# Attention terms as columns of the node products, and separate buffers for the right relational weights

## The chip, the core and the metric

The kernel runs on one core of a Trainium2 chip. The metric is the time of one execution on the device in microseconds (us). The engines are PE (TensorE, matrix products; PEld its weight loads), DVE (VectorE), ACT (ScalarE), POOL (GpSimd) and SP (SyncE, which here only issues DMAs). All engines work side by side from instruction queues of their own and wait for each other by semaphores.

## The reference

Four graph layers follow one another on 6250 nodes with 128 features and 100000 edges sorted by destination; after each the input is added and the rows are normalised.

```
x = layernorm(x + L0(x))            # sum over edges, two linear layers
x = layernorm(x + L1(x))            # attention, two layers:
    h = x @ W_node + b_node
    for l in 0, 1:
        g = h @ lyr_W[l]
        s = (g * att_src[l]).sum(-1);  d = (g * att_dst[l]).sum(-1)
        e = leaky_relu(s[src] + d[dst])          # src, dst with a loop for each node
        h = softmax-weighted sum over edges of g[src] + lyr_bias[l]
x = layernorm(x + L2(x))            # relational, R = 4 relations, H = 4 heads, H * C = 512:
    xl = einsum('nf,rfh->nrh', h, W_l) + b_l     # "left"
    xr = einsum('nf,rfh->nrh', h, W_r) + b_r     # "right"
    e_feat = edge_attr @ W_e[r, :16] + rel_emb[r] @ W_e[r, 16:]     # r = type of the edge
    score = (leaky_relu(xl[src, r] + xr[dst, r] + e_feat) * att[r]).sum(-1)
    softmax over edges, sum of messages, feed-forward layer
x = layernorm(x + L3(x))            # graph convolution
```

## The kernel before, in words

The nodes are 49 blocks of 128 (`NB` = 49, `NP` = 6272 padded nodes), each block with nodes on the 128 partitions. The program is a series of stages (`nc.Block()`); in each, every engine gets a piece of code of its own, and a barrier stands between stages: the next one begins when the slowest engine of the last is through, waits for its DMAs included. Nothing reorders instructions; each engine runs them as they are written.

The attention layers. `gat_input` computes h: `cols_tensor` transposes the rows of x block by block into two PSUM banks, DVE (`cols_vector`, L410) and ACT (`cols_scalar`, L417) copy the groups of four alternately into `cols`, then PE multiplies 49 blocks by W_node (L426) and DVE adds the bias (L709). `gat_nodes`, called for each of the two layers, does the same with h and the layer's weights, ACT copying the products out (L434). Then DVE multiplies g by one attention vector (L761) and sums each row (L764), and again for the other vector: four passes over 6272 columns. SP stores g to the table in HBM (L735, rows of 130 elements of which 128 are g), and once DVE has made the `tail` (a one and the term s, L766) a second DMA stores these two columns (L737). `split_vector` (L1049, L1052) splits d into three bf16 parts. `gat_edges` then gathers table rows for 1664 pairs of an edge tile and a node block (POOL, L810), and `gat_layer` mixes the sums with g.

The relational tables. `rel_tables` makes two tables in HBM, left and right, each with 49 blocks of 4 x 516 columns: per relation 512 columns of the product and 4 of a linear term (the product with attention already summed over a head). Per block PE does four products of 512 columns (L1142, five banks in turn) and a small one (L1147), DVE adds the bias into one of two row buffers `rel_out` (L1249, L1252), and SP stores the buffer (L1110); DVE waits for the store of two blocks earlier before it writes. The left and the right side use the same SBUF places `wl` and `bl` for weights and biases. ACT's queue loads them (L1160, L1161): the left ones after the gates' exponential, the right ones when all left blocks are through and after the **attribute chain**, a loop over 16 edge features in which ACT loads one row of `edge_attr`, casts it to three bf16 parts (L1179) with POOL taking the remainders (L1120), and stores four rows (L1164). Before its first block DVE prepares small things: three-part splits of attention and edge weights, `rel_wide`, the softmax of the gates, the type rows (L1226, L1231), and the linear terms of weights and bias (L1236, L1238). Between the sides it adds four folded rows to the right bias (L1223; PE's L1133) and makes the linear terms again.

The gathers that read both tables (L1702) belong to the next stage, whose first DMA issue is SP's L1719.

## Time and profile before

| what | value |
| --- | --- |
| median of 3 executions | 10470.95 us (10433.81 to 10505.31) |
| the profiled execution | 10493.45 us, of which the span from first to last instruction is 10491.6 us |
| busy | PE 5383.1 us (51%), PEld 3542.6 (34%), DVE 5196.6 (50%), ACT 1919.2 (18%), POOL 5653.5 (54%) |
| granted TensorE clock, mean | 0.697 of full speed |

A row of the timeline has the start in us from the start of the span, the duration in us, the engine (PEq, ACTq, SPq for what a queue issues), the line of the program, the operation, what it writes and reads, and how many of them are merged into the row; in square brackets stands the idle time before it and what ended it. The page of the profile says that matmuls are pipelined and their ends modelled, and that a few matmul records can be missing.

### The profile page before, as it was taken

Reading aid. Unit: us, or ns where it says so; the run is one execution under the profiler, and the core shown is the slowest. Engines: PE = TensorE matmul, PEld = TensorE weight load, DVE = VectorE, ACT = ScalarE, POOL = GpSimd, SP = SyncE. Lnnn points to the kernel's source line nnn. Section 1 sums busy time; section 2 is a strip of 40 time slices with the busy share of each in tenths; the row PEclk is TensorE's granted clock in tenths of the full one; section 3 lists DMA queues with packets and bytes.
Section 4 is the critical chain, followed back from the end, with each engine's and each line's share of the span. In section 5 each row is a group of like instructions: output and inputs, shape, how many; then the busy total and the mean of one; then the engine's idle time right before and its main releaser. Section 6 shows DMA issues by size and latency. Waiting matters only on the chain. (4 is left out here: it accounts for less than half of the span.)

```text
span 10491.6 us, 95206 instructions
## 1 busy us (share of the span) xinstructions
PE 5383.1 (51%) x23693; PEld 3542.6 (34%) x23809; DVE 5196.6 (50%) x19168; ACT 1919.2 (18%) x4711; POOL 5653.5 (54%) x5712
## 2 busy tenths in 40 slices
PE   2333423333332333337777777777767777723333
PEld 2332312223231232223322222222236767613233
DVE  3232443333352333356667777777766666623225
ACT  0000111111111111111022222222224444410000
POOL 6666235555426555521066666666656666356663
PEclk5555655555565555558888898899988888855555
DMA  2111021121121122117566666666656666311111
GB/s 62 46 46 47 20 46 50 54 56 53 54 46 52 55 56 56 53 34 280 231 210 204 201 207 206 202 201 204 202 156 175 176 175 175 94 49 46 46 46 35
DMA packets 445514, 1155.74 MB, mean 110 GB/s; under 512 B 117604, under 2 KB 159172, under 8 KB 431928
## 3 DMA queue, kind: packets, MB, share of 16 engines
q0 software_dynamic: 295984, 849.83, 28.2%
q1 hardware_dynamic: 133660, 272.06, 7.7%
q10 hardware_dynamic: 15340, 27.77, 0.8%
q8 instruction: 213, 3.49, 0.1%
q14 instruction: 317, 2.60, 0.1%
HBM read 1016.71 MB, written 132.52 MB: 110 GB/s over the span
## 5 line engine op out<-in xcount | busy, mean ns | idle before, releaser
L810 POOL DMA_INDIRECT gat_ring<-gat_table,psrc_idx x1664 | 1604.6, 964 | 1804.8 <-PE bank L863 674.3
L863 PE MATMUL bank<-gat_ring,gat_hot 128*128 128x130 f32 x3328 | 759.6, 397 | 1092.2 <-DVE gat_hot L968 707.9
L565 DVE TENSOR_TENSOR acc<-acc,bank 128x129 f32 (+1 forms) x1664 | 479.0, 288 | 1540.2 <-remote 811.4
L1702 POOL DMA_INDIRECT pair<-right_table,idx_r_idx x782 | 799.7, 1023 | 654.9 <-POOLq L1095 217.5
L979 DVE TENSOR_TENSOR acc<-acc,bank 128x130 f32 x1664 | 481.3, 289 | 1225.3 <-remote 682.0
L1852 POOL DMA_INDIRECT msg<-left_table,pidx_idx x832 | 814.4, 979 | 495.5 <-PE bank L1926 203.9
L863 PEld LDWEIGHTS bank<-gat_ring,gat_hot 128*128 128x128 f32 x3328 | 648.8, 286 | 1197.2 <-DVE gat_hot L968 701.7
L1702 POOL DMA_INDIRECT acc<-left_table,idx_l_idx x782 | 804.5, 1029 | 452.0 <-issue 228.7
L511 POOL DMA_INDIRECT gcn_sum_ring<-gcn_table,src_idx x782 | 761.2, 973 | 391.3 <-issue 220.5
L511 POOL DMA_INDIRECT gin_sum_ring<-in_x,src_idx x782 | 761.1, 973 | 381.5 <-issue 221.8
L1764 ACT ACTIVATE positive<-acc 128x512 f32<-128x512 f32 x782 | 492.5, 630 | 2121.1 <-DVE acc L1792 1415.9
L1741 PE MATMUL bank<-pair,ident 128*128 128x512 f32 x1564 | 869.1, 639 | 0.7
L537 PE MATMUL bank<-gcn_sum_ring,gcn_sum_hot 128*128 x1664 | 425.8, 430 | 759.4 <-issue 305.8
L1792 DVE TENSOR_TENSOR acc<-acc,bank 128x512 f32<-128x512 f32 x782 | 532.1, 681 | 479.7 <-remote 233.5
L537 PE MATMUL bank<-gin_sum_ring,gin_sum_hot 128*128 x1664 | 415.8, 422 | 664.0 <-issue 273.1
L1804 DVE CUSTOM_DVE_ANT_0 positive<-positive,bank 128x128 f32<-128x128 f32 x3128 | 711.9, 277 | 42.4 <-issue 38.9
L1738 PE MATMUL bank<-edge_w,feat 128*128 128x512 bf16 x2254 | 680.7, 411 | 49.4 <-DVE acc L1792 23.4
L537 PEld LDWEIGHTS bank<-gcn_sum_ring,gcn_sum_hot 128*128 128x128 f32 x1664 | 357.8, 313 | 827.3 <-issue 826.0
L537 PEld LDWEIGHTS bank<-gin_sum_ring,gin_sum_hot 128*128 128x128 f32 x1664 | 350.4, 307 | 729.3 <-issue 728.3
L833 PE MATMUL bank<-gat_d_parts,gat_spread 128*128 x1664 | 207.9, 184 | 622.1 <-DVE gat_spread L891 333.1
L875 ACT ACTIVATE gat_ring<-gat_ring,gat_wt 128x129 f32<-128x129 f32 x1664 | 491.4, 389 | 3.4 <-issue 2.3
L870 ACT ACTIVATE gat_wt<-gat_sl 128x52 f32<-128x52 f32 x32 | 7.9, 246 | 2621.1 <-DVE gat_ratio L950 2308.8
(499 smaller groups left out, 9587.3 us busy)
## 6 DMA issues: line engine op xcount, KB each, us to landing
gat_place<-local_rows SPq DMA_DIRECT2D x128, 416.0 KB
left_table<-rel_out SPq DMA_DIRECT2D x49, 1032.0 KB, 5.0
right_table<-rel_out SPq DMA_DIRECT2D x49, 1032.0 KB, 3.9
feat<-attr_rows SPq DMA_DIRECT2D x194, 256.0 KB
gat_ring<-gat_table,psrc_idx POOLq DMA_INDIRECT x1664
types<-type_rows SPq DMA_DIRECT2D x98, 256.0 KB
msg<-left_table,pidx_idx POOLq DMA_INDIRECT x832
gin_sum_ring<-in_x,src_idx POOLq DMA_INDIRECT x782
```

What stands on the lines that cost most here:

```text
L511: e.indirect_dma_start(ring[:, at:at + F], None, table[:, :], bass.IndirectOffsetOnAxis(ap=ed["src"][:, i:i + 1], axis=0)).then_inc(*got[b ...
L537: e.matmul(k.psum[j % NBANK][:, 0:width], hot[b % NH][:, j % Q * P:(j % Q + 1) * P], ring[:, bass.ds(at[j % BATCH], width)], start=True, s ...
L810: e.indirect_dma_start(ring[:, at:at + TROW], None, table[:, :], bass.IndirectOffsetOnAxis(ap=ed["psrc"][:, i:i + 1], axis=0)).then_inc(*g ...
L863: e.matmul(k.psum[i % NBANK][:, 0:TROW], hot[i // HQ % NH][:, i % HQ * P:(i % HQ + 1) * P], ring[:, at:at + TROW], start=True, stop=True). ...
L875: e.mul(row, row, wt[:, i % CT:i % CT + 1]).then_inc(*scaled.up())
L1702: e.indirect_dma_start(to[j % NG][:, n * LROW:(n + 1) * LROW], None, tab[:, :], bass.IndirectOffsetOnAxis(ap=idx[:, i:i + 1], axis=0)).the ...
L1738: e.matmul(x, m, edge_w[:, q * LROW:q * LROW + HC], start=(q == 0), stop=False)
L1741: e.matmul(x, c["ident"][:, :], side(rights, i), start=False, stop=True).then_inc(*edge_made.up())
L1764: e.activation(positive[i % NA][:, :], side(lefts, i), ACT.Relu, scale=0.8).then_inc(*relued.up())
L1792: e.tensor_tensor(xs, xs, k.psum[bank_x[i % NX]][:, 0:HC], ALU.add).then_inc(*summed.up())
L1804: d = e.tensor_tensor_reduce(out=pos[:, s], in0=pos[:, s], in1=k.psum[bank_a[at % NE]][:, s], scale=1.0, scalar=0.0, op0=ALU.mult, op1=ALU ...
L1852: e.indirect_dma_start(rows[j % NG][:, n * LROW:(n + 1) * LROW], None, left[:, :], bass.IndirectOffsetOnAxis(ap=ed["pidx"][:, i:i + 1], ax ...
```

## The change

In the attention layers the input product disappears as a stage: in layer 0 a folded matrix `whole` = W_node x [lyr_W, 0, lyr_W a_src, lyr_W a_dst] is made on chip (a transposition, two small products and copies), and x itself is multiplied by it. In both layers the two attention terms are columns of the same product, which has 131 columns for a block (`GROW`: g, a one from the `base` row, s, d). Products go into four banks in groups of three blocks, DVE moves them out with the base row added, and SP stores each group of three blocks with all 130 columns when it is out. The four passes, the ACT copies and the tail are gone. `gx` takes the place of `h` and has rows of 131 elements; the later passes read g, s and d out of it.

In `rel_tables` the right weights and biases get buffers of their own, those of the softmax of the next stage (`soft`), and SP's queue loads them at the start. The left weights are issued by ACT as its first instructions, left bias and attention row by SP as its first. DVE makes the left linear terms and begins with the blocks; everything else that it prepared stands now between the blocks (`between`), at the block numbers written there, and the two sides follow each other without a gap.

```diff
-                e.wait_ge(*taken.at(len(GROUPS)))
-                e.dma_start(tv[:, :, 0:F], blocks3(g)).then_inc(*stored.up(16))
-                e.wait_ge(*tailed.at(1))
-                e.dma_start(tv[:, :, F:TROW], t3).then_inc(*stored.up(16))
-                e.wait_ge(*stored.at(2, 16))
+                for j, (lo, hi) in enumerate(THREES):
+                    e.wait_ge(*taken.at(j + 1))
+                    e.dma_start(tv[lo:hi].rearrange("b p f -> p b f"), g3[:, lo:hi, 0:TROW]).then_inc(*stored.up(16))
+                e.wait_ge(*stored.at(len(THREES), 16))
...
+                if layer == 0:
+                    e.wait_ge(*loaded.at(len(loads), 16))
+                    e.transpose(k.psum[4][:, 0:P], wn[:, :], c["ident"][:, :]).then_inc(*wn_turned.up())
+                cols_tensor(e, k, c, x, turned, out_v, out_s, xw)
+                e.wait_ge(*widened.at(1))
+                if layer == 0:
+                    e.matmul(k.psum[5][:, 0:GROW], bn[:, :], wx[:, :], start=True, stop=True)
+                    e.matmul(k.psum[4][:, P:P + GROW], wn[:, :], wx[:, :], start=True, stop=True).then_inc(*folded.up())
+                    e.wait_ge(*whole_in.at(1))
...
+                for j, (lo, hi) in enumerate(THREES):
+                    if j >= 4:
+                        e.wait_ge(*taken.at(j - 3))
+                    for b in range(lo, hi):
+                        m = e.matmul(k.psum[j % 4][:, (b - lo) * GROW:(b - lo + 1) * GROW], cols[:, b * P:(b + 1) * P],
+                                     weight[:, :], start=True, stop=True)
+                    m.then_inc(*product.up())
...
-                for j in (0, 1):
-                    e.wait_ge(*dve.now())
-                    e.tensor_tensor(blocks3(cols), blocks3(g), att[:, j * F:(j + 1) * F].unsqueeze(1).to_broadcast(
-                        [P, NB, F]), ALU.mult).then_inc(*dve.up())
-                    e.wait_ge(*dve.now())
-                    e.tensor_reduce(nd(j), blocks3(cols), AX_X, ALU.add).then_inc(*dve.up())
+                e.wait_ge(*loaded.at(len(loads), 16))
...
+                cols_vector(e, k, cols, turned, out_v)
...
+        weight = [by_r(wl), [b[:, :] for b in (soft.near01, soft.near, soft.far, soft.pen)]]
+        bias = [by_r(bl), [b[:, :] for b in (soft.val, soft.top, soft.tot, soft.ex)]]
...
+                for dst, src in first_loads:
+                    e.dma_start(dst, src).then_inc(*firsts.up(16))
                 for dst, src in loads:
                     e.dma_start(dst, src).then_inc(*loaded.up(16))
+                for dst, src in later_loads:
+                    e.dma_start(dst, src).then_inc(*laters.up(16))
...
-                    for r in range(R):
-                        e.dma_start(wl[:, r * HC:(r + 1) * HC], w[wn][r]).then_inc(*weights.up(16))
-                    e.dma_start(bl[:, :], broadcast_row(w[bn].rearrange("r f -> (r f)"))).then_inc(*weights.up(16))
...
+                def between(n):
+                    if n == 1:
+                        e.wait_ge(*loaded.at(len(loads), 16))
+                        e.tensor_copy(part(0, SLOTS), typ_i).then_inc(*typed.up())
+                        e.wait_ge(*typed.now())
+                    if n == 2:
+                        gates()
+                    if 3 <= n < 3 + R:
+                        is_type(n - 3)
+                    if n == 8:
+                        split_vector(e, att_f[0:R, 0:HC], att_f[0:R, HC:2 * HC],
+                                     lambda j: att_parts[0:R, j * HC:(j + 1) * HC], dve, att_split)
...
+                    for r in range(R):
+                        if n == FOLD(r) + 1:
+                            e.wait_ge(*laters.at(2 * R, 16))
+                            e.wait_ge(*fold.at(r + 1))
+                            e.tensor_tensor(bias[1][r], bias[1][r], k.psum[7][:, 0:HC], ALU.add).then_inc(*folded.up())
+                        if n in (FOLD(r) + 2, FOLD(r) + 3):
```

Here `FOLD(r)` is 20 + 5r, and n counts the blocks of both sides, 0 to 97.

How the order on the engines moves is seen at three places. The first is DVE from the end of the normalisation before the attention layers to the first instruction of the edge stage of layer 0. Before:

```order
L410 COPY gat_in_cols<-bank 128x512 x6
L410 COPY gat_in_cols<-bank 128x128
L709 TENSOR_TENSOR gat_h<-bank,gat_in_b 128x512 x12
L709 TENSOR_TENSOR gat_h<-bank,gat_in_b 128x128
L685 UNCONDITIONAL_BRANCH
L753 UNCONDITIONAL_BRANCH
L755 MEMSET gat_tail 128x98
L410 COPY gat_cols<-bank 128x512 x6
L410 COPY gat_cols<-bank 128x128
L761 TENSOR_TENSOR gat_cols<-gat_h,gat_att 128x6272
L764 TENSOR_REDUCE gat_node<-gat_cols 128x49
L761 TENSOR_TENSOR gat_cols<-gat_h,gat_att 128x6272
```

After the change, from the first instruction of the node stage on (`ISA` is the reduction of a product of two rows, with the store of its sum):

```order
L749 COPY gat_whole<-gat_bn 128x128
L751 COPY gat_wn<-bank 128x128
L752 COPY gat_bn<-gat_whole 128x128
L755 ISA gat_scratch,gat_w<-gat_w,gat_att 128x128
L755 ISA gat_w 128x1
L755 ISA gat_scratch,gat_w<-gat_w,gat_att 128x128
L755 ISA gat_w 128x1
L413 COPY gat_cols<-bank 128x512 x6
L413 COPY gat_cols<-bank 128x128
L761 TENSOR_TENSOR gat_base<-gat_base,bank 128x131
L762 COPY gat_whole<-bank 128x131
L766 TENSOR_TENSOR gat_g<-bank,gat_base 128x393 x16
```

The seven copies, thirteen additions and the four full passes of the input and node stages have gone; seven copies and seventeen additions out of PSUM stay, and in front of them stand the preparations. The second place is SP in the same node stage of layer 0, first before, then after:

```order
L733 DMA gat_w<-in_L_gnn_lyr_W 128x128
L733 DMA gat_att<-in_L_gnn_att_src 128x128
L733 DMA gat_att<-in_L_gnn_att_dst 128x128
L733 DMA gat_bias<-in_L_gnn_lyr_bias 128x128
L735 DMA gat_table<-gat_h 128x49x128
L737 DMA gat_table<-gat_tail 128x49x2
```

```order
L707 DMA gat_w<-in_L_gnn_lyr_W 128x128
L707 DMA gat_att<-in_L_gnn_att_src 128x128
L707 DMA gat_att<-in_L_gnn_att_dst 128x128
L707 DMA gat_bias<-in_L_gnn_lyr_bias 128x128
L707 DMA gat_wn<-in_L_gnn_W_node 128x128
L707 DMA gat_bn<-in_L_gnn_b_node 128x1
L710 DMA gat_table<-gat_g 128x3x130 x16
L710 DMA gat_table<-gat_g 128x130
```

The two stores behind everything have become 17, one for each group of three blocks, and there are two more loads. The third place is DVE at the start of the relational tables, from the column copies on. Before:

```order
L1204 TENSOR_REDUCE gate<-gate 128x1
L1206 TENSOR_SCALAR gate<-gate 128x4
L1208 TENSOR_REDUCE gate<-gate 128x1
L1210 RECIPROCAL gate<-gate 128x1
L1212 TENSOR_SCALAR gate<-gate 128x4
L1214 TENSOR_SCALAR gate<-gate 128x4
L1226 CAST attr_parts<-rel_out 128x896
L1231 TENSOR_SCALAR attr_parts<-attr_parts 128x896 x4
L1236 TENSOR_TENSOR rel_out<-rel_wl,att_all 128x2048
L1238 TENSOR_REDUCE w_lin<-rel_out 128x16
L1236 TENSOR_TENSOR rel_out<-rel_bl,att_all 128x2048
L1238 TENSOR_REDUCE b_lin<-rel_out 128x16
```

After:

```order
L413 COPY acc<-bank 128x512 x6
L413 COPY acc<-bank 128x128
L1267 TENSOR_TENSOR rel_out<-rel_wl,att_all 128x2048
L1268 TENSOR_REDUCE w_lin<-rel_out 128x16
L1267 TENSOR_TENSOR rel_out<-rel_bl,att_all 128x2048
L1268 TENSOR_REDUCE b_lin<-rel_out 128x16
L1282 TENSOR_TENSOR rel_out<-bank,rel_bl 128x512 x4
L1285 TENSOR_TENSOR rel_out<-bank,b_lin 128x4x4
L1228 CAST attr_parts<-soft_code 128x896
L1282 TENSOR_TENSOR rel_out<-bank,rel_bl 128x512 x4
L1285 TENSOR_TENSOR rel_out<-bank,b_lin 128x4x4
L1210 TENSOR_REDUCE gate<-gate 128x1
```

Between the column copies and the first block only the linear terms are left; type rows and gates stand behind blocks 0, 1, 2 and so on. At the change of sides DVE had, before, the rows L1223 to L1238 below between block 48 and block 49:

```order
L1249 TENSOR_TENSOR rel_out<-bank,rel_bl 128x512 x4
L1252 TENSOR_TENSOR rel_out<-bank,b_lin 128x4x4
L1223 TENSOR_TENSOR rel_bl<-rel_bl,bank 128x512 x4
L1236 TENSOR_TENSOR rel_out<-rel_wl,att_all 128x2048
L1238 TENSOR_REDUCE w_lin<-rel_out 128x16
L1236 TENSOR_TENSOR rel_out<-rel_bl,att_all 128x2048
L1238 TENSOR_REDUCE b_lin<-rel_out 128x16
L1249 TENSOR_TENSOR rel_out<-bank,rel_bl 128x512 x4
L1252 TENSOR_TENSOR rel_out<-bank,b_lin 128x4x4
```

Those pieces stand now singly behind blocks 20 to 37, and the first right block follows the last left one.

## Rows read from the trace of the kernel before

**Rows 1.** Timeline around layer 0's input and node stages; columns as explained above.

```profile
1382.56 0.33 SPq L688 DMA_DIRECT2D gat_in_b<-in_L_gnn_b_node  x1
...
1415.32 11.46 PE L426 MATMUL bank<-gat_w,gat_cols 128*128 128x128 f32 x98 [0.43 <-DVE gat_cols L410]
...
1427.33 6.69 DVE L761 TENSOR_TENSOR gat_cols<-gat_h,gat_att 128x6272 f32<-128x6272 f32 x1 [12.11 <-ACT gat_h L434]
...
1464.43 29.83 SPq L819 DMA_DIRECT2D gat_place<-local_rows  x6
```

**Rows 2.** Timeline, node stage of layer 1 and the passes ahead of it.

```profile
3042.60 6.68 DVE L1028 TENSOR_TENSOR acc<-acc,gat_node 128x6272 f32<-128x6272 f32 x1
...
3063.01 0.33 SPq L733 DMA_DIRECT2D gat_w<-in_L_gnn_lyr_W  x1
...
3064.18 0.69 DVE L410 COPY gat_cols<-bank 128x512 f32<-128x512 f32 x1 [0.93 <-PE bank L402]
...
3073.42 0.29 DVE L410 COPY gat_cols<-bank 128x128 f32<-128x128 f32 x1 [0.42 <-PE bank L402]
...
3085.82 0.38 SPq L735 DMA_DIRECT2D gat_table<-gat_h  x1
...
3122.66 12.65 SPq L819 DMA_DIRECT2D gat_place<-local_rows  x5
```

**Rows 3.** Timeline of the relational tables, edges and change of sides.

```profile
4739.27 1.31 SPq L1099 DMA_DIRECT2D score<-in_L_gnn_W_e  x2
...
4753.54 0.41 DVE L1049 CAST att_parts<-score 4x512 bf16<-4x512 f32 x1 [3.57 <-DMA rel_out<-in_recs]
...
4762.56 0.17 DVE L1214 TENSOR_SCALAR gate<-gate 128x4 f32<-128x4 f32 x1
...
4770.24 6.16 PE L1142 MATMUL bank<-rel_wl,acc 128*128 128x512 f32 x8 [20.59 <-DMA rel_bl<-in_L_gnn_b_l]
...
4774.18 2.28 DVE L1236 TENSOR_TENSOR rel_out<-rel_wl,att_all 128x2048 f32<-128x2048 f32 x1
...
4774.66 0.47 ACTq L1173 DMA_DIRECT2D score<-in_attr  x1
...
4784.98 2.48 DVE L1249 TENSOR_TENSOR rel_out<-bank,rel_bl 128x512 f32<-128x512 f32 x4
...
4976.63 0.17 DVE L1252 TENSOR_TENSOR rel_out<-bank,b_lin 128x16 f32<-128x16 f32 x1
...
5018.06 1.79 ACTq L1160 DMA_DIRECT2D rel_wl<-in_L_gnn_W_r  x4
...
5045.28 2.48 DVE L1249 TENSOR_TENSOR rel_out<-bank,rel_bl 128x512 f32<-128x512 f32 x4
...
5224.90 0.16 DVE L1252 TENSOR_TENSOR rel_out<-bank,b_lin 128x16 f32<-128x16 f32 x1
5229.51 0.60 SPq L1719 DMA_DIRECT2D types<-type_rows  x1
```

**Rows 4.** Windows: stretch, length, busy by engine, PEclk, DMA share, GB/s.

```profile
3067.00:3068.00 1.00, 1.00 (x6) 0.97 (x7) 0.02 (x1) 0.52 (x1) 0.00 (x0) 0.50 0.27 22
3102.00:3103.00 1.00, 0.00 (x0) 0.00 (x0) 1.00 (x1) 0.00 (x0) 0.00 (x0) 0.50 0.53 84
4765.00:4767.00 2.00, 0.00 (x0) 0.00 (x0) 0.00 (x0) 0.00 (x0) 0.00 (x0) 0.50 1.00 385
4785.00:4881.00 96.00, 92.74 (x245) 42.97 (x246) 63.63 (x124) 15.20 (x19) 20.05 (x12) 0.98 0.89 340
5137.00:5225.00 88.00, 87.38 (x240) 41.61 (x238) 67.38 (x122) 0.00 (x0) 0.00 (x0) 1.00 0.70 289
```

**Rows 5.** DMA to landing, tiles left_table, then right_table (in the tables' stage).

```profile
DMA to landing us min/median/max: 3.9/5.0/8.5
...
DMA to landing us min/median/max: 3.9/3.9/5.3
```

**Rows 6.** DMA issues, 4739 to 4785: count, KB each, median us to landing.

```profile
type_rows<-attr_parts ACTq DMA_DIRECT2D x5, 224.0 KB, 1.9
```

More of the change, by code:

```diff
@@ L33 @@
 LROW = HC + H
+GROW = F + 3
 LAG = 3
@@ L989, in _, with gat_layer @@
                     sums(cn)
-def gat_layer(k, c, ed, w, layer, g, x, acc, table, local_rows):
+def gat_layer(k, c, ed, w, layer, gx, x, acc, table, local_rows):
     name = f"gat{layer}"
@@ L997, in gat_layer @@
         stat = k.sb("ln1_stat", 3 * NB, ctx=own)
-        gat_nodes(k, c, w, layer, g, node, d_parts, bias, table)
+        gat_nodes(k, c, w, layer, gx if layer else x, gx, node, d_parts, bias, table)
         gat_edges(k, c, ed, name, acc, table, local_rows, d_parts)
         acc3, nd = blocks3(acc, ROW), lambda j: node[:, j * NB:(j + 1) * NB]
-        s, d, has, loop, high, w_loop, w_sum, total = (nd(j) for j in range(8))
+        g3 = blocks3(gx, GROW)[:, :, 0:F]
+        s, d = (blocks3(gx, GROW)[:, :, F + j] for j in (1, 2))
+        has, loop, high, w_loop, w_sum, total = (nd(j) for j in range(2, 8))
         dve, compared, exped = k.begin("dve", "compared", "exped")
```

392 lines of the change are left out of this document (193 added, 199 removed).

## Prediction, made before the changed kernel was run

> **What bounds the kernel now.** I read the row of busy times first, then the timeline at the edges of the stages, then windows and landing times. Over the whole span of 10491.6 us no engine is busy more than 54% of the time (the table of the section on time and profile): the kernel is a line of stages, each closed by a barrier, and a stage's length is set by its own last wait. The page's chain of waits covers only the last stage, so it says nothing about these two places, and they have to be read from the timeline. The profiled execution took 10493.45 us against a median of 10470.95; the sum below is made against 10493.45 and carried over to the median as a ratio.
>
> Three stretches are touched. **First**, input product and node stage of attention layer 0: from SP's first issue at 1382.56 to the first issue of the edge stage at 1464.43, 81.9 us [rows 1]. The reader is to see that after the last product VectorE makes four full passes of 6.69 us, the first at 1427.33, and only then can SP store the last two columns, in pieces of 8 bytes; the stage ends some 10 us after that. **Second**, the same node stage of layer 1: 3063.01 to 3122.66, 59.7 us [rows 2]. **Third**, the relational tables: 4739.27 to 5229.51, 490.2 us [rows 3]. There the left side's 49 blocks run from 4784.98 to 4976.8, 3.91 us each, and the right side's from 5045.28 to 5225.07, 3.67 each. Before the first block stand 45.7 us, and between the sides 68.5 us in which VectorE and TensorE mostly idle: the right weights may only be fetched (5018.06) when ScalarE's chain over the edge attributes is through, because the same engine queues both and the weights go into the place of the left ones.
>
> **Part 1, attention layers.** Removed: the whole input product, the four passes (4 x 6.69 = 26.8 us on the path, both layers), the ScalarE copies and the tail store. Added: loads ahead of the column copies (VectorE waits for them before its first copy), two reductions of 128 columns, in layer 0 a transposition and a fold of two matrices, three more columns in each product, and 17 stores instead of two. What the store waits for is new: it may begin after three blocks and then runs beside the products.
>
> Layer 0, step by step. Four loads issued from 3063.01 had their traffic over by about 3067.6 (the window 3067 to 3068 still shows a share of 0.27, [rows 4]): 4.6 us. Two more cost some 0.9 us, so the weights are in at 1382.56 + 5.5 = 1388.1. Transposing, copying and the two reductions are seven short instructions in a line, at 0.17 to 0.41 us each [rows 3] some 2.2 us: 1390.3. From the first column copy to the last takes 3073.42 - 3064.18 = 9.24 us [rows 2] and 0.36 more to the first product: 1399.9. The fold adds two small matmuls, two evictions and two handoffs, 1.2 us: 1401.1. Products: 98 half products in 11.46 us [rows 1], times 131/128, 11.7 us; three blocks take 0.72 us and their eviction of 393 columns 0.56 (0.69 us for 512 columns, 0.29 for 128, [rows 2]), so TensorE still sets that pace. The first store goes out 1.3 us after the first product, at 1402.4. Now the store: the single one of layer 1 was issued at 3085.82 [rows 2] and its traffic ended within the window 3102 to 3103 [rows 4], 16.7 us. That is longer than the 11.7 us of the products, so **the store is what comes late next**: 1419.1, plus 2.4 us from the end of traffic to the next stage (4.4 us from the last right block to 5229.51, less 2 us of data, [rows 3]): 1421.5. Gain 1464.43 - 1421.5 = **43 us**.
>
> Layer 1 has no fold and four loads: 3067.6 + 0.9 = 3068.5 for the first copy (4.3 us later than now), 3078.1 first product, 3079.4 first store, 3096.1 end of traffic, 3098.5 next stage. Gain 3122.66 - 3098.5 = **24 us**. Together 67 us. Bounds: 75 if the products set the end instead of the store (2 x 5 us less, some of it lost in the last landing), 57 if loads and fold take 5 us more in each layer. The later elementwise passes read rows 131 elements apart instead of 128; a pass over `acc`, whose rows are 130 apart, takes what the others do (6.68 and 6.69 us, [rows 2]), so I put that at nothing.
>
> The Trainium skill (SBUF — State Buffer, The DMA setup-cost knee) speaks against the 17 stores: each transfer pays a roughly fixed 2 us, so one should send the largest single transfer. By the fit that it gives, 195 KB would take 2.5 us and 17 of them in a line 42 us, an estimate; overlap between stores in one queue decides it, and the rows of this stage show no two stores in flight of this size, so neither case is ruled out by them.
>
> **Part 2, relational tables.** Three things move. (a) *The start.* VectorE's work before the first block was 9.2 us of splits and gates (4753.54 to 4762.7) after 3.57 us of waiting, then a wait for weights until 4770.1, then 4.1 us of type rows, then 10.8 us of linear terms [rows 3]. Now only the linear terms stay, four passes of 2.29 us, and the left weights are issued first. 3.1 MB have to be in (weights, biases, attention row); at the 385 GB/s of [rows 4] that is 8.1 us after a first issue near 4740, 4750.4 with the landing, about when the column copies end (4749.97: the cast at 4753.54 had waited 3.57 us). First eviction at 4750.5 + 4 x 2.29 + 0.3 = 4760.0 instead of 4784.98: **25 us**. (b) *The gap between the sides* of 68.5 us goes altogether, if the right weights are in: they are issued before the first table store. (c) *What comes back.* The attribute chain starts when block 6 does, near 4783 instead of 4774.66, and needs about 250 us (243.4 us for its sixteen features now, the last three without company, [rows 3]), so it ends near 5035. Blocks beside it cost 3.91 us, blocks without it 3.67: the share of the DMA engines is 0.89 in the one window and 0.70 in the other [rows 4], the landing of a table store 5.0 us against 3.9 in the middle [rows 5]. That makes 70 blocks at 3.91 and 28 at 3.67, 376.5 us, against 371.6 for all 98 now: 5 us back. The work moved between the blocks is 9.2 + 2.2 us from the start, and for the right terms 4 x (0.69 + 4 x 0.69) = 13.8 us: 25 us of VectorE in about 20 pieces of at most 2.8 us. Its cover is the wait for the store two blocks back: a block holds 2.65 us of VectorE work in 3.91. Pieces of 1.4 us hide but for some 0.2, the three of 1.6 to 2.8 us stick out by about 1.5 each; with four fold matmuls of 1.1 us on TensorE I charge 5 us. If the cover were gone it would be the full 25 us and 4.4 more.
>
> SP has three small stores put ahead of block 10's; they are issued while SP waits for that block anyway. ScalarE waits for the gates until block 2, and behind that wait stands the attribute chain, counted under (c). POOL's part of that chain follows it and holds nobody else: the next stage's gathers wait for the barrier.
>
> Sum: blocks end at 4760.0 + 376.5 + 5 = 5141.5, the next stage begins 4.4 us later at 5146, against 5229.51: **83 us**. Bounds 58 (cover gone) and 92 (no inserts seen, chain not slower).
>
> Total 67 + 83 = **150 us**: 10493.45 - 150 = 10343.5, or 1.43%. On the median: 10470.95 x (1 - 150/10493.45) = **10321 us**.
>
> **Rivals.**
> *The work between blocks is not covered.* For it: left blocks already wait on stores, so a late VectorE makes a late store, and the loop over two buffers passes it on. Against it: 1.26 us free in each block. It costs 25 + 4.4 - 5 = 24 us more: gain 126, 10345 us. Chance 0.12.
> *The 17 stores follow one another.* A small store of 224 KB landed in 1.9 us [rows 6]; with 0.38 us to issue, 17 x 2.28 = 38.8 us instead of 16.7, 22 us in each layer: gain 106, 10365 us. Against it: the loads at the start of the third stretch are issued two in 1.31 us, without waiting for each other [rows 3], and such loads flow at 385 GB/s [rows 4]. This is where the skill's rule would lead. Chance 0.06.
> *More is gained.* The products and not the store end the node stages, and the chain slows fewer blocks: 75 + 92 = 167 and up, 10304 us. Chance 0.09.
> *Slower than before.* Place: the loop over the two row buffers. A pair of blocks takes landing + issue + VectorE's 2.65 us; at 5.0 us that is (5.0 + 0.32 + 2.65)/2 = 3.98 each, as seen. If the new company (right weights, the chain, short pieces) raised the landing of every table store to the 8.5 us of the slowest one now [rows 5], it would be 5.7 us a block, 562 us for 98, 185 more than the 377 above: 35 us slower than before, 10506 us. It decides against the change from a landing of 7.8 us on. Against it: the same bytes are written at the same rate, and the extra 2 MB of weights are in before the second block. Chance 0.03.
> *The change does not do what it says*, in that the right side still waits: its wait is for weights landed 200 us earlier and terms made ten blocks earlier, so this has no price that I can find and is held in the last case.
>
> **How the numbers follow.** Forecast 0.70, the rivals as given. Single executions of this kernel lie from 10433.81 to 10505.31, 0.35% about the median, so about 1% is what a measurement can tell from no change. The forecast's own range is 125 to 175 us; with the scatter of 0.3% on top and the first three rivals inside it, 10275 to 10380. Faster by over 1% needs 105 us: all of the forecast save its edge, most of the first rival, half of the second: 0.85. Within 1%: 0.12. Slower: 0.03.
>
> **What would show it.** After it the edge stage of layer 0 begins near 1421, 39 us after the stage's first issue; VectorE has no pass of 6.69 us between products and edges; store traffic runs unbroken for about 17 us. The node stage of layer 1 is about 35.5 us long. The first eviction of the left table stands 21 us after the stage's first issue, the 98 blocks run without a gap and the stage is 407 us long. Wrong would be: a traffic record with holes between the 17 stores, blocks 8 to 14 and 20 to 38 longer than their neighbours by more than 1 us, or a first column copy later than 8 us into the node stages.

## The result, and the profile after

The changed kernel takes 10348.08 us (median of 4 executions, 10303.08 to 10355.34) against 10472.08 us (median of 4) for the kernel before: a ratio of 0.9874 with a 95% interval of 0.983 to 0.9918, that is 124 us or 1.26% faster. The interval is clear of 1. The forecast was 10321 us, faster by over 1% with a chance of 0.85. The profiled execution took 10344.3 us (the sum of the prediction, made against 10493.45, gave 10343.5).

Busy times from the page of the changed kernel, against the table of the section on time and profile:

```profile
span 10342.5 us, 94979 instructions
PE 5314.2 (51%) x23667; PEld 3474.6 (34%) x23667; DVE 5146.7 (50%) x19201; ACT 1901.7 (18%) x4679; POOL 5637.5 (55%) x5712
```

They say as little as before: 69 us less work on PE and 50 on DVE, and 149 us less span. The timeline at the edges of the stages tells more. Node stage of layer 0, to be laid beside [rows 1] (columns as there):

```profile
1377.09 0.33 SPq L707 DMA_DIRECT2D gat_w<-in_L_gnn_lyr_W  x1
1382.82 0.22 DVE L749 COPY gat_whole<-gat_bn 128x128 f32<-128x128 f32 x1 [5.32 <-issue]
1384.48 0.69 DVE L413 COPY gat_cols<-bank 128x512 f32<-128x512 f32 x1
1393.92 0.29 DVE L762 COPY gat_whole<-bank 128x131 f32<-128x131 f32 x1
1394.26 11.21 PE L730 MATMUL bank<-gat_whole,gat_cols 128*128 128x131 f32 x98 [0.59 <-DVE gat_whole L762]
1395.31 10.75 DVE L766 TENSOR_TENSOR gat_g<-bank,gat_base 128x393 f32<-128x393 f32 x17 [1.10 <-PE bank L730]
1395.90 13.59 SPq L710 DMA_DIRECT2D gat_table<-gat_g  x17
```

The four passes of 6.69 us are gone; products, evictions and the issuing of 17 stores run side by side. The edge stage begins at 1415.62: 38.5 us after the first issue, where it was 81.9. Windows of the same stretch (after the busy times: clock, DMA share, GB/s):

```profile
1397.00:1412.00 15.00, 8.47 (x76) 8.28 (x75) 8.82 (x20) 0.00 (x0) 0.00 (x0) 0.85 1.22 201
1413.00:1414.00 1.00, 0.00 (x0) 0.00 (x0) 0.00 (x0) 0.00 (x0) 0.00 (x0) 0.50 0.46 86
1414.00:1416.00 2.00, 0.00 (x0) 0.00 (x0) 0.00 (x0) 0.36 (x1) 0.00 (x0) 0.50 0.03 7
```

Store traffic starts within 1396 to 1397 and ends within 1413 to 1414, about 17 us, and the stage ends 2 us later. (A share above 1 can't be right, so I use the GB/s.) Layer 1, beside [rows 2]:

```profile
3028.20 0.33 SPq L707 DMA_DIRECT2D gat_w<-in_L_gnn_lyr_W  x1
3033.26 0.06 DVE L747 MEMSET gat_w<- 128x1 f32 x1 [4.65 <-DMA gat_bias<-in_L_gnn_lyr_bias]
3033.90 0.69 DVE L413 COPY gat_cols<-bank 128x512 f32<-128x512 f32 x1
3045.42 12.85 SPq L710 DMA_DIRECT2D gat_table<-gat_g  x17
3065.23 0.81 SPq L822 DMA_DIRECT2D gat_place<-local_rows  x2
```

37.0 us long. Relational tables, beside [rows 3]:

```profile
4710.77 0.33 SPq L1114 DMA_DIRECT2D rel_bl<-in_L_gnn_b_l  x1
4722.76 0.29 DVE L413 COPY acc<-bank 128x128 f32<-128x128 f32 x1 [0.42 <-PE bank L404]
4725.01 2.29 DVE L1267 TENSOR_TENSOR rel_out<-rel_wl,att_all 128x2048 f32<-128x2048 f32 x1 [1.95 <-DMA rel_wl<-in_L_gnn_W_l]
4734.30 2.48 DVE L1282 TENSOR_TENSOR rel_out<-bank,rel_bl 128x512 f32<-128x512 f32 x4
4736.95 0.33 SPq L1130 DMA_DIRECT2D left_table<-rel_out  x1
4933.15 5.90 SPq L1130 DMA_DIRECT2D right_table<-rel_out  x2
5010.52 4.15 ACTq L1180 DMA_DIRECT2D attr_rows<-attr_parts  x4
5118.17 0.59 SPq L1752 DMA_DIRECT2D types<-type_rows  x1
```

407.4 us long. There is no gap between the sides: the first right store stands 196.2 us after the first left one, which is 49 blocks of 4.00 us. One block stands out. The prediction named blocks 8 to 14 longer than their neighbours by more than 1 us as a sign of being wrong, and block 8 is: its store follows that of block 7 by 8.08 us, where each of the four distances before is 3.66.

```profile
4762.76 0.32 SPq L1130 DMA_DIRECT2D left_table<-rel_out  x1
4770.84 0.32 SPq L1130 DMA_DIRECT2D left_table<-rel_out  x1
```

What VectorE did there is read further down. All stretches of the two profiled executions, from the first DMA issue of one to that of the next:

| stretch | before | after | difference | forecast |
| --- | --- | --- | --- | --- |
| up to the first attention stage (not touched) | 1382.6 | 1377.1 | -5.5 | 0 |
| input and node stage, layer 0 | 81.9 | 38.5 | **-43.3** | -43 |
| edges and mixing, layer 0 (row distance only) | 1598.6 | 1612.6 | +14.0 | 0 |
| node stage, layer 1 | 59.7 | 37.0 | **-22.6** | -24 |
| edges, mixing and norm, layer 1 (row distance only) | 1616.6 | 1645.5 | +28.9 | 0 |
| relational tables | 490.2 | 407.4 | **-82.8** | -83 |
| the rest (not touched) | 5262.1 | 5224.3 | -37.8 | 0 |

The three touched stretches give 148.7 us. The open question is in the other rows. Are the 43 us more in the edge stages and the 38 us less behind the tables scatter, or do they belong to the change?

### The profile page after: what moved, and what is told of

Read it like the earlier page. It is cut to its first block and busy times, and to the rows that moved or that the text cites. A ratio compares the mean times of both kernels' runs of the same rounds, so it can differ in the third digit from the quotient of the medians.

```text
span 10342.5 us, 94979 instructions
## 1 busy us (share of the span) xinstructions
PE 5314.2 (51%) x23667; PEld 3474.6 (34%) x23667; DVE 5146.7 (50%) x19201; ACT 1901.7 (18%) x4679; POOL 5637.5 (55%) x5712
## 5 line engine op out<-in xcount | busy, mean ns | idle before, releaser
L866 PE MATMUL bank<-gat_ring,gat_hot 128*128 128x130 f32 x3328 | 730.0, 385 | 975.6 <-DVE gat_hot L971 574.1
L866 PEld LDWEIGHTS bank<-gat_ring,gat_hot 128*128 128x128 f32 x3328 | 622.1, 275 | 1077.2 <-DVE gat_hot L971 572.4
L1837 DVE CUSTOM_DVE_ANT_0 positive<-positive,bank 128x128 f32<-128x128 f32 x3128 | 711.3, 278 | 40.7 <-issue 38.9
L1771 PE MATMUL bank<-edge_w,feat 128*128 128x512 bf16 x2346 | 705.3, 413 | 38.4 <-DVE acc L1825 24.9
```

What stands on the lines that cost most here:

```text
L866: e.matmul(k.psum[i % NBANK][:, 0:TROW], hot[i // HQ % NH][:, i % HQ * P:(i % HQ + 1) * P], ring[:, at:at + TROW], start=True, stop=True). ...
L1771: e.matmul(x, m, edge_w[:, q * LROW:q * LROW + HC], start=(q == 0), stop=False)
L1837: d = e.tensor_tensor_reduce(out=pos[:, s], in0=pos[:, s], in1=k.psum[bank_a[at % NE]][:, s], scale=1.0, scalar=0.0, op0=ALU.mult, op1=ALU ...
```

## The experiments

The runs were made in groups, each on one chip with the kernel before beside it: in the table the first four rows, the next four, the next three, and the last row alone. The first three groups fell on two chips on which the kernel before takes 8585 to 8597 us, the last on a third where it takes 10471 us, much as in the result above. So the runs are compared by stretches and by their own group's ratio. The stretches are in us, all from profiled executions; three runs have a single execution, so they are read by their traces alone:

| run | node 0 | edges 0 | node 1 | edges 1 | tables | rest | ratio (95% interval) |
| --- | --- | --- | --- | --- | --- | --- | --- |
| before again | 84.5 | 1141.0 | 61.5 | 1174.0 | 494.8 | 4419.3 | one execution, 8579.14 us |
| changed again | 40.9 | 1141.0 | 38.9 | 1175.8 | 413.0 | 4422.4 | 0.9822 (0.9807 to 0.9837) |
| attention part alone | 41.4 | 1141.6 | 40.2 | 1173.8 | 495.2 | 4421.2 | 0.993 (0.9917 to 0.9944) |
| tables part alone | 83.8 | 1143.7 | 61.6 | 1174.5 | 410.0 | 4430.1 | 0.9898 (0.9883 to 0.9914) |
| one store | 47.0 | 1141.6 | 46.5 | 1174.1 | 410.8 | 4425.8 | 0.9847 (0.9832 to 0.9862) |
| steps ahead of the blocks | 38.1 | 1140.1 | 36.4 | 1173.3 | 420.6 | 4432.8 | 0.9841 (0.9826 to 0.9856) |
| chain later | 38.4 | 1140.9 | 36.8 | 1172.3 | 454.4 | 4435.8 | one execution, 8484.05 us |
| half rows | 38.1 | 1140.1 | 37.3 | 1173.4 | 394.8 | 4427.5 | 0.981 (0.9796 to 0.9823) |
| no linear product | 37.5 | 1139.6 | 36.2 | 1173.2 | 399.0 | 4439.9 | one execution, 8434.56 us |
| columns first | 32.7 | 1138.6 | 31.4 | 1172.7 | 409.1 | 4433.0 | 0.9813 (0.98 to 0.9827) |
| columns first and half rows | 31.8 | 1136.9 | 31.7 | 1174.0 | 395.6 | 4427.3 | 0.9799 (0.9785 to 0.9812) |
| a pad in each block (slower chip) | 38.6 | 1595.1 | 37.7 | 1646.4 | 418.3 | 5220.7 | 0.9884 (0.9864 to 0.9905) |

### Does the change touch anything outside its three stretches?

The kernel before again, the changed kernel again, and each half of the change alone (only `rel_tables` exchanged between the two programs):

> The kernel before once more, for a second profile of it: how far do the stages that nobody touched scatter from one execution to the next? Theory A (the change acts in three stages alone): the edge stage of layer 0 with its mixing passes takes 1598.6 us or differs from that by as much as it did after the change (+14), the same for the edge stage of layer 1 (1616.6, +29 after the change) and for all that follows the tables (5262.1, -38 after the change). Rival B (the change also lengthens the edge stages, 43 us, and something gives it back later): both edge stages come within 5 us of the first profile, 1598.6 and 1616.6. The three touched stretches are to be 81.9, 59.7 and 490.2 us, within 1 us, by both.

> The changed kernel once more. Theory A: the three touched stretches repeat at 38.5, 37.0 and 407.4 us within 1 us each, and the untouched ones move by some 10 to 40 us without a pattern, so that 148.7 us of the three stretches against the 124 us between the medians is scatter. Rival B: edge stages at 1612.6 and 1645.5 again within 5 us, that is 43 us longer than before.

> The attention part alone: the node stages of the change with the relational tables of the kernel before. Theory A, parts add: 43.3 + 22.6 = 66 us faster than before, ratio 0.9937, tables stretch 490 us. Rival B, the attention part costs something in the edge stages (rows 131 apart, other places in the memory): 66 - 43 = 23 us faster, ratio 0.998.

> The relational part alone: the tables of the change with the node stages before. Theory A: 83 us faster, ratio 0.9921, node stretches 81.9 and 59.7 us as before. Rival B (later stages win 38 us from the tables part, by what they find in the memory or in the queues): 83 + 38 = 121 us, ratio 0.988.

On this chip the edge stages agree to 0.0 and 1.8 us between before and changed, 1141.04 against 1141.04 and 1174.02 against 1175.79. So neither the row distance of 131 instead of 128 nor anything else in the change costs more there than these 2 us. The touched stretches gain 43.6 + 22.5 + 81.8 = 148 us, what they gained on the other chip, and the medians 8596.75 - 8443.28 = 153.5 us. The halves add: 61.5 us and 88.0 us by their medians, 149.5 together, against 66 and 83 expected. My expectation that the three stretches repeat within 1 us was too narrow: they came out 1.9 to 5.6 us longer. The figures expected for the edge stages could not be met, since these stages are 440 to 460 us shorter on this chip, with either kernel. Rival B is out on this chip. On the slower chip the pad run below has 1595 us in the edge stage of layer 0, so the +14 us there are scatter. But it again has 1646 us in the edge stage of layer 1 and 5221 us behind the tables, as the changed kernel had and the kernel before not. With one profile of before at that speed I can't tell whether the +29 and -38 us belong to the change there. They cancel but for some 10 us.

### What ends the node stages?

One store of the whole table in place of 17 (the last wait, for one store instead of 17, is not shown):

```
-for j, (lo, hi) in enumerate(THREES):
-    e.wait_ge(*taken.at(j + 1))
-    e.dma_start(tv[lo:hi].rearrange(...), g3[:, lo:hi, 0:TROW])
+e.wait_ge(*taken.at(len(THREES)))
+e.dma_start(tv.rearrange("b p f -> p b f"), g3[:, :, 0:TROW])
```

> The changed kernel with one store of the whole table in each attention layer, after the last product, in place of 17. Theory A (the store is what ends the node stage, and its 17 pieces flow without a gap beside the products): the store goes out some 11 us later, right after the last product is taken, still takes some 17 us, and each node stage is 10 to 12 us longer, 20 to 24 us in all. Rival B (each transfer pays a fixed 2 us and the 17 pieces wait for one another): the single store moves its 3.3 MB in some 9 us at the 385 GB/s that loads reached, and the stages stay within 3 us or get shorter. By the Trainium skill (SBUF - State Buffer, The DMA setup-cost knee) the 17 pieces would need an estimated 42 us against some 10 us for the single one.

Timeline of that run, SP's queue:

```profile
1229.14 0.38 SPq L709 DMA_DIRECT2D gat_table<-gat_g  x1
1247.23 0.81 SPq L821 DMA_DIRECT2D gat_place<-local_rows  x2
```

The single store goes out 10.8 us after the first product was taken (1218.37) and the next stage begins 18.1 us later. With 17 stores the same distance, first store to next stage, is 19.7 us (1395.90 to 1415.62) and 19.8 us in layer 1. So the 3.3 MB take nearly the same time in one piece or in 17, and what 17 pieces buy is the earlier start: against the three other runs of this group, whose node stages are the change's (38.1 to 38.4 and 36.4 to 37.3), the stages are 8.6 to 8.9 and 9.2 to 10.1 us longer, a little under the expected 10 to 12. The pieces did not wait for one another. By the Trainium skill (SBUF — State Buffer, The DMA setup-cost knee), which gives each transfer a roughly fixed 2 us, 17 pieces in a line would have been the slower form by some 30 us, an estimate from its figures. The traces do not agree: 17 pieces took 19.7 us against 18.1, so in one queue the fixed parts overlap.

Then the loads. Their wait stood ahead of the column copies (5.3 us in layer 0, 4.65 in layer 1). Here the copies go first, and the widening stands between the fifth and the sixth of VectorE's (TensorE's part of the edit is not shown):

```
 def cols_vector(e, k, cols, turned, out_v, inside=None):
     for g, (lo, hi) in enumerate(GROUPS):
+        if inside and g == 10:
+            inside()                  # wait for the loads, widen the weights
```

> The changed kernel with the column copies of both attention layers ahead of the wait for the loads: VectorE copies five groups and widens the weights between the fifth and the sixth, TensorE transposes the node weight after group 8. Theory A (loads and copies then run side by side, and the chain up to the first product is what sets the first store, the stores' 17 us the end): first product some 4 us earlier in both layers, the stages 4 us shorter each, 8 us in all. Rival B (the copies' own pace is broken by the steps between them): under 2 us in all.

SP's queue in that run, layer 0:

```profile
1203.52 0.33 SPq L711 DMA_DIRECT2D gat_w<-in_L_gnn_lyr_W  x1
1217.08 13.05 SPq L714 DMA_DIRECT2D gat_table<-gat_g  x17
1236.19 0.81 SPq L830 DMA_DIRECT2D gat_place<-local_rows  x2
```

The first store goes out 13.6 us into the stage instead of 18.8, and the next stage begins 19.1 us behind it, near the 19.7 of the change. The stages are 32.7 and 31.4 us long, 4.8 us less each than in the run of its group whose node stages are the change's (37.5 and 36.2): theory A, with a little more than the 4 us expected.

### What sets the pace of the blocks?

The prediction took the round of two row buffers for it: a buffer is free again when its store has landed, so a block takes (landing + issue + VectorE's work) / 2. Four runs test this, three here and the pad of the next section. The first holds the attribute chain until the left side is done (ScalarE waits for the last left eviction ahead of `for f in range(DE)`):

> The changed kernel with ScalarE's chain over the edge attributes held until the left side's last block is done. Theory A (the chain is what makes a left block longer than a right one): left blocks fall from 3.98 to 3.74 us or below, right blocks rise to some 3.95 us; the chain then needs some 255 us from there and ends the stage, about 55 to 70 us later than now. Rival B (it is the left table, or its early loads): left blocks stay at 3.98 and right ones at 3.74.

The page's landings of the table stores in that run:

```profile
left_table<-rel_out SPq DMA_DIRECT2D x49, 1032.0 KB, 3.9
right_table<-rel_out SPq DMA_DIRECT2D x49, 1032.0 KB, 5.0
```

and the windows of a left stretch without the chain and a right one with it (busy PE, PEld, DVE, ACT, POOL, then clock, DMA share, GB/s):

```profile
3650.00:3790.00 140.00, 140.00 (x379) 65.98 (x378) 117.09 (x217) 0.00 (x0) 0.00 (x0) 1.00 0.69 285
3820.00:3900.00 80.00, 74.94 (x198) 34.35 (x198) 51.65 (x100) 12.16 (x15) 16.72 (x10) 0.98 0.87 334
```

The sides have changed roles: left 185.3 us (3.78 a block, with the steps between the blocks in it), landing 3.9; right 3.97 a block, landing 5.0. So the chain, not the side, makes a block slow. The stage grew by 44 us against the 410.8 of its group, not 55 to 70, since the chain alone took some 245 us, not 255. And the first window shows what I had not read: **TensorE is busy 140.00 of 140 us.** Without the chain the blocks are bound by TensorE. The kernel before had it in a row that stands ahead of the prediction: 87.38 of 88 us in its last window [rows 4].

To test that, the small product of the linear terms is left out of all blocks but two (`if n < 2:` ahead of it), and with it TensorE's wait for its bank and VectorE's wait for the product. The other blocks' linear columns are then read from products of block 0 or 1.

> The changed kernel without the 16-column product of the linear terms in all blocks but the first two (left out: the linear terms of the other blocks' rows, whose evictions read the product of block 0 or 1 again, so what stands in those columns of the tables is not the reference's). It takes some 0.3 us of TensorE's work out of each block and nothing of VectorE's, SP's or the stores'. Theory A (in blocks without company TensorE is what sets the pace, busy 100% of the window): right blocks fall from 3.64 us, where nothing runs beside them, to 3.35 to 3.5. Rival B (the prediction's account: the round of two row buffers sets it, (landing + issue + VectorE's work) / 2): 3.64 us stay.

SP's queue over the last right blocks, this run:

```profile
3900.09 88.73 SPq L1130 DMA_DIRECT2D right_table<-rel_out  x27
```

and its window there:

```profile
3905.00:3985.00 80.00, 79.82 (x187) 35.19 (x186) 62.82 (x120) 0.00 (x0) 0.00 (x0) 1.00 0.76 315
```

With the product, in the run with columns first, whose tables are those of the change, the queue:

```profile
3900.02 84.00 SPq L1138 DMA_DIRECT2D right_table<-rel_out  x24
```

and the window:

```profile
3905.00:3980.00 75.00, 75.00 (x207) 35.87 (x206) 57.38 (x104) 0.00 (x0) 0.00 (x0) 1.00 0.70 289
```

26 distances in 88.4 us are 3.40 us a block, 23 in 83.7 us are 3.64. Less work for TensorE makes a block 0.24 us shorter at the same buffers and the same stores: theory A. The round of the buffers, by the prediction's formula 3.44 us at the landing of 3.9 on this side, is then just as near, so 3.40 alone does not tell which of the two limits is left. Beside the chain the same cut brought little: the left side took 195.9 us against 199.3, that is 0.07 us a block, and TensorE was busy 128.73 of 140 us there (window 3640 to 3780).

The third gives the buffers more room: each row stored in two halves, from four half buffers in the same memory. The cut is shortened. Not shown are the small product, which moves ahead of the four others, its eviction, which is done in two, and the wait for one half buffer at a time.

```
+for half in range(2):
+    at = slice(half * 2 * LROW, (half + 1) * 2 * LROW)
     e.wait_ge(*biased...); e.wait_ge(*lin_biased...)
-    e.dma_start(tview[b], out_rows[n % 2][:, :])
+    e.dma_start(tview[b][:, at], out_rows[n % 2][:, at])
```

> The changed kernel with each block's row stored in two halves of two relations each (4 half buffers in the same memory, 196 stores of 516 KB in place of 98 of 1032 KB; the product of the linear terms goes ahead of the four others, its eviction is done in two). Theory A (the blocks are bound by the round of two buffers, landing plus VectorE's work, not by the rate of the DMA engines): a block comes near VectorE's own work, 3.0 to 3.4 us, and the stage is 50 to 85 us shorter. Rival B (writing at some 270 GB/s is what the memory takes beside the rest): within 5 us. Rival C (196 stores pay more fixed cost): some us longer.

The stage is 394.8 us long, 16 us shorter than its group's 410.8: neither A's 50 to 85 nor B's 5. The window of its left side:

```profile
3640.00:3780.00 140.00, 138.48 (x372) 64.00 (x371) 121.25 (x256) 23.60 (x28) 30.46 (x19) 1.00 0.95 353
```

TensorE is busy 99% beside the chain, where it was 97.31 of 100 us in the changed kernel and 96.32 in the one before (windows 4800 to 4900). The left side, beside the chain, gains most: 186.5 us against 199.2 in the run with one store, 0.26 us a block. Once the stores let go, TensorE's 3.64 us a block is what is left; 98 of them are 357 us, and this run's two sides take 186.5 + 180.9 = 367.4. I had expected VectorE's own work to be the floor; it is not the next limit. The run changed the order of the products too, and no run tells the two apart.

### Are the steps between the blocks covered?

VectorE's steps of blocks 1 to 19 ahead of block 0 (`for n in range(20): between(n)`):

> The changed kernel with VectorE's steps that stand between blocks 1 and 19 (the wait for all loads, gates, type rows, both splits) put ahead of the first block again. Theory A (between the blocks they hide behind the wait for the row buffer): the first table store comes 15 to 20 us later, the blocks take as long as before, and the stage is 12 to 18 us longer. Rival B (between the blocks they were not covered): the first blocks get shorter by what the start loses, and the stage is within 4 us of the changed kernel's.

The first table store comes 15.7 us later (40.8 us into the stage instead of 25.1), both sides together are 5.9 us shorter than in the run with one store, whose tables are unchanged (379.8 against 385.7), and the stage is 9.8 us longer, below the 12 to 18 expected. Part of the 5.9 us is another matter: the type rows are ready sooner, so the chain starts at +28 us instead of +44 and keeps company to fewer blocks. Only 1.2 us of the 5.9 are gained on the left side, where the steps had stood, and 4.7 on the right, where none had. So the run bounds the uncovered part of these steps at some 6 us but doesn't measure it, and it says nothing of the steps of blocks 20 to 37.

The run with the chain later shows all of them at once, without company. Its left side, from the first left store to the first right one, takes 185.3 us where 49 blocks of 3.66, the distance at which most of them stand, are 179.3. So the steps cost 6.0 us. Most of that is not VectorE's: the stores of blocks 20, 25, 30 and 35 each follow the one before by 4.81 us, and there TensorE makes a fold product between the blocks:

```profile
3686.91 1.12 PE L1158 MATMUL bank<-rel_we,rel_wide 8*128 8x512 f32 x2
```

Each of these groups of five blocks takes 1.1 us more than five times 3.66, so the four fold products come to 4.5 us, and everything else between the blocks to 1.5. TensorE was busy through the whole of that side (180.00 of 180 us, window 3617 to 3797).

Beside the chain it is another matter at block 8, where VectorE splits the attention row into three parts. In the changed kernel, with GpSimd's subtraction for the chain:

```profile
4762.58 1.66 POOL L1140 TENSOR_TENSOR score<-score,attr_parts 128x782 f32<-128x782 f32 x1 [218.08 <-ACT attr_parts L1195]
4762.60 1.91 DVE L1054 CAST att_parts<-score 4x512 bf16<-4x512 f32 x1
4765.27 1.87 DVE L1054 CAST att_parts<-score 4x512 bf16<-4x512 f32 x1
```

and with the chain later:

```profile
3643.70 0.40 DVE L1054 CAST att_parts<-score 4x512 bf16<-4x512 f32 x1
```

The split took 5.7 us instead of 2.7, and block 8's store came 8.08 us behind block 7's instead of 5.12. This is where the prediction's sign was seen, and it was there in all seven profiles that have the split beside the chain and rows stored whole (7.9 to 8.4 us). Blocks 20 to 38 can't be read this way: beside the chain neighbouring distances scatter from 2.5 to 7.1 us even in the kernel before, which has no steps there.

To measure the cover itself, one more VectorE pass in each of the 98 blocks:

```
+then(e.tensor_tensor(soft.parts[:, 0:256], att_all[:, 0:256], att_all[:, 0:256], ALU.mult))
 if n >= 2:
     e.wait_ge(*stored[n % 2].at(n // 2, 16))
```

> The changed kernel with one more VectorE product of 256 columns (nothing reads it) at the start of each of the 98 blocks, some 0.35 to 0.4 us with its wait, ahead of the wait for the row buffer. It is the cover of the steps between the blocks measured 98 times over. Theory A (TensorE sets 3.65 us a block where nothing else runs, the row buffer's round some 3.98 beside the chain; VectorE has 0.6 us free in either): the stage stays within 6 us of the changed kernel's 411 to 413 us. Rival B (steps between the blocks are not covered): 98 x 0.37 = 36 us longer, blocks at 4.0 and 4.3 us.

Windows of that run, a left and a right stretch:

```profile
4800.00:4900.00 100.00, 92.08 (x239) 41.34 (x238) 86.01 (x158) 16.02 (x19) 20.98 (x13) 0.98 0.85 325
5020.00:5100.00 80.00, 80.00 (x221) 38.15 (x219) 68.85 (x134) 0.00 (x0) 0.00 (x0) 1.00 0.71 292
```

The pad's own row among the groups of the right window:

```profile
L1275 DVE TENSOR_TENSOR soft_parts<-att_all 128x256 f32<-128x256 f32 x22 | 9.1, 416 | 0.0
```

The right side takes 185.2 us as without pads (185.0): where TensorE is busy 80.00 of 80 us, 0.42 us more of VectorE's work per block cost nothing. The left side takes 207.7 us, against 196.2 in the changed kernel's first profile and 199.2 to 200.4 in four others of the same tables on the faster chips: 0.15 to 0.23 us a block, a third to a little over half of the pad, and TensorE falls from 97 to 92%. Beside the chain the cover is partial; that a late store makes the next round late there is the likely reason. The stage took 418.3 us. That is 5 to 7 us over the 411 to 413 from which the expectation was made, at the edge of A's 6, and 10.9 over the 407.4 of the result's profile; both are far from B's 36.

### The version the runs point to

> Columns first and half-row stores together, the version that the runs so far point to. Theory A: the gains add, 8 us of the node stages and 16 to 18 us of the tables, some 25 us faster than the changed kernel and 178 us faster than the one before. Rival B: one of them is lost in the scatter, 155 to 165 us.

Columns first and half rows together: 8417.79 us against 8592.4, a ratio of 0.9799 (0.9785 to 0.9812), 174.6 us faster than before, where the changed kernel was 153.5 us faster in its group and theory A had put 178. Its stretches are 31.8, 31.7 and 395.6 us, so 459 us for the three against 493 in the changed kernel's own run. It is the fastest of all that ran, though its interval overlaps those of its two halves.

## Why the prediction was right

- **Node stage, layer 0, 43 us**: measured 43.3. First column copy 7.4 us into the stage (forecast 7.7), first product 17.2 (18.5), first store 18.8 (19.8), next stage 38.5 (38.9). The step on which it rests, the store comes late next at the same length of traffic, is shown by the run with one store.
- **Layer 1, 24 us**: measured 22.6. Store traffic and tail took 19.8 us rather than 19.1, and the first store came 0.8 us later.
- **17 stores flow together**: shown; the rival by which they follow one another is out.
- **Tables, 83 us**: measured 82.8, but from terms that were off against each other, and that they came so near is luck. The first eviction came 23.5 us into the stage, not 21, since VectorE waited 1.95 us for the left weights after column copies that themselves ended at 12.3, not 10.7. Blocks with all steps between them took 379.5 us from first eviction to the last, against 381.5. The sum also counts 70 blocks beside the chain, where its own times (4783 to 5035) cover only 64; that makes 1.4 us.
- **The reason given for the blocks was half wrong.** "The loop over two buffers passes it on" holds beside the chain. Without the chain TensorE sets 3.64 us. The formula gave 3.98 on the left "as seen"; on the right the same formula gives (3.9 + 0.32 + 2.65) / 2 = 3.44 against 3.67, and I didn't work it out. The number came out because 3.67 was taken from the trace, not from the formula. It is also why the rivals were mis-stated: VectorE's work between blocks is free where nothing runs beside them and in part paid for beside the chain.
- **Charge for the steps between the blocks, 5 us of 25**: of the right size but of other parts. Without company all steps cost 6.0 us, of which the four fold products on TensorE are 4.5 and VectorE's pieces the rest. The prediction's sign of being wrong, a block among 8 to 14 longer by more than 1 us, did appear: block 8 by 4.4 us. It had charged the moved casts at their time without company (0.41 us, [rows 3]), and two of them took 1.9 us.
- **Row distance at nothing**: shown on the faster chip, to 2 us; on the slower one not settled.
- **The median** came out 27 us above the forecast though the profiled sum fit within 1 us. The interval of the result, 86 to 178 us faster, holds both, and the group on the faster chip gave 153.5. The fit within 1 us is luck: the untouched stages moved by -5.5, +14.0, +28.9 and -37.8 us between the two profiles and happened to cancel. I carried the gain over as a ratio, 149.7 us; by the stretches the gain in us was the same at 10470 and at 8590 us (148.7 and 148), so it is an amount, not a share.

## What to carry to other kernels

Read the busy time of every engine in the window of a repeated block before naming what paces it: one that is busy all of the time is the first suspect, even where a formula for the store's round comes near the measured pace, and a run with less work for it decides. Where a barrier closes a stage, let the last transfer start with its first finished piece, and put waits for loads behind work that doesn't need them. What hides work between blocks is the engine that is the bound there; the same step can be free in one half of a loop and in part paid for in the other.

## What the runs showed that I had not expected

- The same program took some 10470 us on one chip and 8597 us on another, 18% less, while the touched stretches were equal within 5 us (81.9 and 84.5, 59.7 and 61.5, 490.2 and 494.8). The difference is in the gather stages: edges of layer 0 1598.6 against 1141.0 us. One gather took nearly the same there, but the idle time ahead was twice as long. The rows of the kernel before, from its first profile and then from the faster chip:

```profile
L810 POOL DMA_INDIRECT gat_ring<-gat_table,psrc_idx x1664 | 1604.6, 964 | 1804.8 <-PE bank L863 674.3
```

```profile
L810 POOL DMA_INDIRECT gat_ring<-gat_table,psrc_idx x1664 | 1628.2, 979 | 914.3 <-issue 485.2
```

  The cause stays open; the granted clock over these gathers was 0.56 and 0.63 on average (windows 1470 to 3000 and 1290 to 2400), nearer the lower of its two levels (1.2 GHz, a share of 0.5) on both chips.
- A small VectorE cast took four times as long beside GpSimd's elementwise work, as at block 8 above. In the run with the steps ahead, one cast of 516 columns three times, and GpSimd's subtractions:

```profile
3620.15 0.43 DVE L1054 CAST edge_w<-score 128x516 bf16<-128x516 f32 x1
3620.65 2.18 POOL L1140 TENSOR_TENSOR score<-score,attr_parts 128x782 f32<-128x782 f32 x1 [139.56 <-ACT attr_parts L1195]
3621.35 1.77 DVE L1054 CAST edge_w<-score 128x516 bf16<-128x516 f32 x1
3623.79 1.66 POOL L1140 TENSOR_TENSOR score<-score,attr_parts 128x782 f32<-128x782 f32 x1 [0.95 <-ACT attr_parts L1195]
3623.88 1.85 DVE L1054 CAST edge_w<-score 128x516 bf16<-128x516 f32 x1
```

  The one cast that ended before GpSimd started took 0.43 us; the two beside it took 1.77 and 1.85 us and ended within 0.3 us of the end of the subtraction beside them (3622.83 and 3625.45). With the chain later, casts of both kinds took 0.40 to 0.43 us; that run takes ScalarE's part and the DMAs of the chain away too, not GpSimd's alone. The Trainium skill (SBUF — State Buffer, Who interferes with whom) says that a cast in its faster mode and a GpSimd instruction want one pair of ports, and that the later one waits until the other is through; these rows agree. The cast is not alone in it: in the pad run the subtraction of block 8's split, with both inputs in SBUF, took 2.04 and 2.13 us beside GpSimd instead of 0.68, while the blocks' additions out of PSUM took 0.68 us beside GpSimd as elsewhere.
- A 3.3 MB store of 520-byte rows moved at some 200 GB/s in one piece or in 17 (201 and 214 in the windows), while the tables' 8256-byte rows went at up to 340 GB/s, and at 353 in halves of 4128 bytes. No run varied the length of a row alone.
